# A graph network on one core: norms two octets ahead in the first pass, and 832 packed gathers in the last

## What is computed

```
deg[n]   = number of edges whose source is n
norm[e]  = edge_weight[e] / sqrt(deg[src[e]] * deg[dst[e]])      # first pass, with guards
h[n]     = sum over edges e with dst[e] == n of norm[e] * x[src[e]]   # pass 1
...      # a second pass in source order, a third over q_table, dense layers, a GRU
fwd[n]   = sum over edges of one direction of fwd_table[src]     # pass over fwd_table, 128 wide
bwd[n]   = sum over edges of the other direction of bwd_table    # last pass, 128 wide
out      = layernorm(sums, residual)                             # last turns
```

## Time and profile before

| | |
|---|---|
| median of 3 runs | 7041.7 us (7039.99 to 7042.25) |
| the profiled execution's own time | 7030.23 us |
| its span, first to last instruction | 7028.5 us |
| mean granted TensorE clock | 0.753 of full speed |
| first pass, first to last gather | 277.0 to 1456.4 us |
| last pass, first to last gather | 5862.1 to 6964.0 us |

### The profile page before, as it was taken

The page is one execution under the profiler, slowest core; times in us unless marked ns, Lnnn a source line. Parts: engine busy times, 40 slices in busy tenths (PEclk is TensorE's granted clock), DMA queues, the critical chain, the costliest instruction groups (busy, mean ns, idle before and its releaser), DMA issues. The chain is left out here.

```text
span 7028.5 us, 109321 instructions
## 1 busy us (share of the span) xinstructions
PE 4886.3 (70%) x21773; PEld 3443.5 (49%) x21774; DVE 4004.0 (57%) x9278; ACT 2212.8 (31%) x4093; POOL 4281.9 (61%) x4466
## 2 busy tenths in 40 slices
PE   5455555679999998998888887994555554555553
PEld 3333333447777775676555555553333333333332
DVE  7766666647777775986777775662332222332224
ACT  3333333438888882014333333540000000000000
POOL 1376666727777774004777775006777777777774
PEclk8577667889999998669999999995555555555555
DMA  3133333334333331333333335112221113221222
GB/s 98 44 100 98 97 97 97 105 99 121 104 103 103 104 103 30 99 126 121 105 105 105 105 105 127 34 31 65 65 64 53 53 53 51 52 52 53 52 53 70
DMA packets 292434, 579.79 MB, mean 82 GB/s; under 512 B 86843, under 2 KB 160903, under 8 KB 292169
## 3 DMA queue, kind: packets, MB, share of 16 engines
q0 software_dynamic: 184128, 466.71, 24.9%
q1 hardware_dynamic: 108168, 111.80, 5.2%
HBM read 534.69 MB, written 49.91 MB: 83 GB/s over the span
## 5 line engine op out<-in xcount | busy, mean ns | idle before, releaser
L887 PE MATMUL bank<-ring,oh 128*128 128x128 f32 x3520 | 910.6, 440 | 1094.5 <-DMA ring<-fwd_table,stage_i 558.2
L887 PEld LDWEIGHTS bank<-ring,oh 128*128 128x128 f32 x3520 | 783.5, 328 | 1355.8 <-issue 1355.8
L613 POOL DMA_INDIRECT ring<-h_table,stage_i x880 | 852.4, 969 | 376.9 <-issue 190.4
L631 POOL DMA_INDIRECT ring<-fwd_table,stage_i x880 | 830.6, 944 | 327.0 <-issue 264.8
L631 POOL DMA_INDIRECT ring<-bwd_table,stage_i x880 | 831.8, 945 | 274.3 <-issue 203.6
L1304 ACT ACTIVATE ring<-big 128x889 f16<-128x889 f16 x840 | 873.9, 1041 | 197.8 <-PE bank L965 161.6
L1876 DVE TENSOR_TENSOR acc<-bank,acc 128x1024 f32 x220 | 269.6, 1225 | 987.1 <-PE bank L887 987.1
L965 PE MATMUL bank<-ring,big 128*128 128x445 f16 (+1 forms) x3360 | 773.8, 352 | 0.0
L915 PE MATMUL bank<-big,oh 128*128 128x257 f32 x1072 | 421.9, 559 | 355.5 <-ACT big L1255 219.1
L661 POOL DMA_INDIRECT big<-x_and_degree,stage_i x536 | 507.9, 948 | 187.7 <-issue 118.1
L954 PE MATMUL bank<-ring,oh 128*128 128x256 f32 x1760 | 563.3, 403 | 55.4 <-DVE oh L1845 51.9
(11 more groups left out here) (452 smaller groups left out, 8379.9 us busy)
## 6 DMA issues: line engine op xcount, KB each, us to landing
acc<-places_in_block SPq DMA_DIRECT2D x74, 384.0 KB, 3.5
ring<-h_table,stage_i POOLq DMA_INDIRECT x880, 2.7
ring<-fwd_table,stage_i POOLq DMA_INDIRECT x880
ring<-bwd_table,stage_i POOLq DMA_INDIRECT x880
big<-x_and_degree,stage_i POOLq DMA_INDIRECT x536, 2.8
h_table<-hq SPq DMA_DIRECT2D x50, 128.0 KB, 1.7
x_table<-ring SPq DMA_DIRECT2D x25, 256.0 KB, 2.1
x_turned<-turned SPq DMA_DIRECT2D x25, 256.0 KB, 2.0
```

The costliest lines, as they stand in the source:

```text
L613: pool.indirect_dma_start(out=gbuf[:, u % RING, 0:width], out_offset=None, in_=table, in_offset=bass.IndirectOffsetOnAxis(ap=stage_i[:, v, ...
L631: pool.indirect_dma_start(out=last_rows[:, u, :], out_offset=None, in_=table, in_offset=bass.IndirectOffsetOnAxis(ap=stage_i[:, v, u % RIN ...
L887: mm = pe.matmul(sums[:, ds(b, 1), :].rearrange("p b f -> p (b f)"), oh[:, place, :], last_rows[:, v * RING + u, :], start=False, stop=Tru ...
```

## The change

Four things are altered.

1. **First pass.** `turn` does products and norms for octet k+2 instead of k+1 during octet k. Two octets are prepared before the first turn, and the last full turn is taken out of the loop, because there the last octet has none behind it. ACT no longer waits, ahead of the pass, for POOL to stage five octets.
2. **Prologue.** Twelve of the out-degree batches are put among the 36 weight transposes on PE, one ahead of every three.
3. **Last pass.** Unpadded rows are gathered, 832 instead of 880, into 64 places (`packed`) which take the spare part of `big` and the first columns of `ring`, now one tensor. Tile t uses row t minus its block number. POOL works out that place for each tile (`place_of_tile`) and how many rows must have landed for each group of four (`rows_needed`) during the GRU stage, with ten operations. PE loads eight more registers for each octet, and reads one number for each group and waits for so many rows. SP relays: for each four gathers it waits for their semaphore and adds four to `rows_landed`, then waits for matmuls and frees the next places (`rows_free`). ACT stages four octets ahead.
4. **Indices of the unpadded order.** SP reads them back with two DMAs, PE turns them in seven transposes and ACT copies them to `d_idx` with two operations, all ahead of the node sums.

```diff
-        ring = sb("ring", [P, 2 * RING * (D + 1)])
+        ring = whole[:, BIG:BIG + 2 * RING * (D + 1)]
+        PLACES = 64
+        SETS, ROW_TURNS = PLACES // GROUP, -(-J * P // P) // PLACES
+        packed = whole[:, NX:NX + PLACES * P].rearrange("p (r f) -> p r f", f=P)
...
+            sp.dma_start(flat_win[:, 0:full, :], by_row[0:full * P, :].rearrange("(g p) n -> p g n", p=P)).then_inc(S["row_win_in"], 16)
+            sp.dma_start(flat_win[0:J - full * P, full, :], by_row[full * P:J, :]).then_inc(S["row_win_in"], 16)
...
+            with sp.Fori(0, ROW_TURNS) as i:
+                for g in range(SETS):
+                    sp.wait_ge(gd[g % RING], i * (GROUP * 16 * SETS // RING) + packed_before(g % RING) + GROUP * 16 * (g // RING + 1))
+                    sp.sem_inc(S["rows_landed"], GROUP)
+                    sp.wait_ge(S["mm"], i * PLACES + before_pass(3) + 8 + g * GROUP)
+                    sp.sem_inc(S["rows_free"], 1)
...
-            gathers_by_groups(bwd_dram, before_pass(3))
+            with pool.Fori(0, ROW_TURNS) as i:
+                for u in range(PLACES):
+                    if u % RING == 0:
+                        pool.wait_ge(S["staged"], i * (PLACES // RING) + STAGED[4] + u // RING + 1)
+                    if u % GROUP == 0:
+                        pool.wait_ge(S["rows_free"], i * SETS + u // GROUP + 1)
+                        apart(pool, S["pool_waited"])
+                    pool.indirect_dma_start(out=packed[:, u, :], out_offset=None, in_=bwd_dram,
+                                            in_offset=bass.IndirectOffsetOnAxis(ap=stage_i[:, u // RING % 4, u % RING:u % RING + 1], axis=0)).then_inc(gd[u // GROUP % RING], 16)
...
             for m, (a, _, _) in enumerate(TURN):
+                if m % 3 == 0:
+                    out_degree_batch(CHUNKS[0] + m // 6, m // 3 % 2)
...
+            def packed_pass(slots, shift):
+                def octet(o, v):
+                    pe.load(regs, slots[0:1, ds(o * RING, RING)])
+                    pe.load(row_regs, place_of_tile[0:1, ds(o * RING, RING)])
...
+                        if u % GROUP == 0:
+                            pe.wait_ge(S["one_hot"], n + GROUP)
+                            needed = pe.value_load(rows_needed[0:1, ds(o * 2 + u // GROUP, 1)], min_val=1, max_val=ROW_TURNS * PLACES)
+                            pe.wait_ge(S["rows_landed"], needed)
+                        b = pe.snap(regs[u], min_val=0, max_val=RING - 1)
+                        row = pe.snap(row_regs[u], min_val=0, max_val=PLACES - 1)
...
-            act.wait_ge(S["first_staged"], WIDE)
...
+            with act.Fori(0, ROW_TURNS * PLACES // (4 * RING) - 1) as i:
+                for v in range(4):
+                    act.wait_ge(S["rows_landed"], i * (4 * RING) + (v + 1) * RING)
+                    stage(d_idx, i * (4 * RING) + (v + 4) * RING, v)
...
-                def turn(i, groups, last, places):
+                def turn(i, groups, last, places, ahead):
                     for h in range(groups):
-                        v, at = (h // 2 + 1) % WIDE, i + (h // 2 + 1) // WIDE
-                        if not last:
+                        v, at = (h // 2 + 2) % WIDE, i + (h // 2 + 2) // WIDE
+                        if h // 2 + 2 < ahead:
                             (edge_norms if h % 2 else degree_products)(at, v)
```

More of the change, by code:

```diff
@@ L161, in build @@
         NX = NBE * D
[L162 removed]
+        BIG = 3 * NBE * D // 2
+        whole = sb("big", [P, BIG + 2 * RING * (D + 1)])
+        big = whole[:, 0:BIG]
         x_sb = big[:, 0:NX].rearrange("p (b f) -> p b f", f=D)
@@ L310, in build @@
         zeros = gate_bc
+        rows_needed = gate_rows[0:1, 0, 0:TILES // GROUP].bitcast(I32)
+        row_scratch = [ring[0:1, TC * k:TC * k + TILES] for k in range(2)]
+        assert E <= ROW_TURNS * PLACES * P <= J * P and PLACES - 4 * GROUP >= NB - 1
         pairs_in = lambda a: a.rearrange("p (k n) -> p k n", n=2 * D)
@@ L740, in _ @@
             regs = [pe.alloc_register(f"pe_blk{j}") for j in range(8)]
+            row_regs = [pe.alloc_register(f"pe_row{j}") for j in range(8)]
             slot_regs = regs + [pe.alloc_register(f"pe_blk{j}") for j in range(8, BATCH)]
             pe.sem_inc(S["mm"], 8)
+            pe.sem_inc(S["rows_free"], 3)
             pe.sem_inc(S["sort_mm"], 3)
@@ L783, in turn_windows, with out_degree_batch @@
                         fills += 1
+            def out_degree_batch(i, k):
+                pe.wait_ge(S["dego_oh"], i * 2 + k + 1)
+                for u in range(BATCH):
+                    mm = pe.matmul(bank[7][:, 0:3 * NP], oh_k[k][:, u, :], prod_k[k][:, u, :], start=False, stop=False, skip_group_check=True)
+                mm.then_inc(S["dego_mm"], 1)
             def out_degrees(first, last):
@@ L788, in out_degrees @@
                     for k in range(2):
[L789 to L792, removed]
+                        out_degree_batch(i, k)
             def join_runs():
@@ L896, in scatter_pass @@
                     octet(FULL_TURNS, v)
+            def packed_pass(slots, shift):
+                def octet(o, v):
+                    sums = octet_sums[(v + shift) % 3]
+                    pe.load(regs, slots[0:1, ds(o * RING, RING)])
+                    pe.load(row_regs, place_of_tile[0:1, ds(o * RING, RING)])
+                    pe.wait_ge(S["accd"], o * RING + before_pass(3) + 4 - 2 * RING)
+                    for h in range(2):
+                        pe.matmul(bank[(v + shift) % 3 * 2 + h][:, :].rearrange("p (b f) -> p b f", f=P), zero_row,
+                                  zero_row.unsqueeze(1).to_broadcast([1, 512 // P, P]), start=True, stop=False, skip_group_check=True)
+                    for u in range(RING):
+                        n = o * RING + before_pass(3) + u
+                        place = (2 * (v + shift) + u // GROUP) % 3 * GROUP + u % GROUP
+                        if u % GROUP == 0:
[4 more added lines that the diff above has]
+                        row = pe.snap(row_regs[u], min_val=0, max_val=PLACES - 1)
+                        mm = pe.matmul(sums[:, ds(b, 1), :].rearrange("p b f -> p (b f)"), oh[:, place, :],
+                                       packed[:, ds(row, 1), :].rearrange("p r f -> p (r f)"), start=False, stop=True, skip_group_check=True)
+                        if u % GROUP == GROUP - 1:
+                            mm.then_inc(S["mm"], GROUP)
+                with pe.Fori(0, FULL_TURNS) as i:
+                    for v in range(3):
+                        octet(i * 3 + v, v)
+                for v in range(REST // RING):
+                    octet(FULL_TURNS * 3 + v, v)
             def turn(n, q, src, b):
@@ L1038, in _ @@
             pe.matmul(bank[4][:, 0:D], ones[0:1, :], staged_x[0:1, 1, :], start=True, stop=True).then_inc(S["pe_chain"], 1)
+            pe.wait_ge(S["row_win_in"], 32)
+            for g in range(TG):
+                n = min(P, J - g * P)
+                mm = pe.transpose(bank[6 if g < 4 else 0][:, g % 4 * P:g % 4 * P + n], row_win[0:n, g, :, 0], ident[0:n, 0:n])
+            mm.then_inc(S["pe_chain"], 1)
             node_sums()
@@ L1944, in first_pass @@
                 edge_norms(0, 0)
+                degree_products(0, 1)
+                edge_norms(0, 1)
                 with dve.Fori(0, EXTRA) as i:
                     chain.enter(i, 19)
-                    turn(i, LONG // GROUP, False, True)
+                    turn(i, LONG // GROUP, False, True, WIDE + 2)
                 chain.leave(EXTRA)
-                with dve.Fori(EXTRA, LONG_TURNS) as i:
+                with dve.Fori(EXTRA, LONG_TURNS - 1) as i:
                     chain.enter(i - EXTRA, 10)
-                    turn(i, LONG // GROUP, False, False)
-                chain.leave(LONG_TURNS - EXTRA)
-                turn(LONG_TURNS, RING // GROUP, True, False)
+                    turn(i, LONG // GROUP, False, False, WIDE + 2)
+                chain.leave(LONG_TURNS - 1 - EXTRA)
+                turn(LONG_TURNS - 1, LONG // GROUP, False, False, WIDE + 1)
+                turn(LONG_TURNS, RING // GROUP, True, False, 0)
                 dve.wait_ge(S["accd"], T + 4)
```

32 lines of the change are left out of this document (27 added, 5 removed).

## The result

The changed kernel takes 6926.25 us (median of 3, 6920.03 to 6926.57) against 7041.7; the ratio is 0.9834 with a 95% interval of 0.9811 to 0.9856. The forecast was 6917 with a range of 6895 to 6945. The profiled execution took 6926.25 us with a span of 6924.5, and there the forecast for an execution like the profiled one was 6905, so 21 us are to be explained; 13.8 of them lie between two profiles of this same kernel and are no part of the change.

The account below looks back on a forecast made before the run. No engine always busy: DVE's late norms stalled POOL in the first pass; POOL's gather count set the last. 7030.2 - 68 + 5.5 - 3.8 + 1.0 - 60.0 + 0.3 = 6905.2; median 6917 us, range 6895 to 6945.

Parts of the forecast that it names:

- prologue, first gather: Prologue: out-degree batches among the transposes cut DVE's 10.80 us stall to about 7, -3.8 us (bounds 0 to -10.8).
- stalls of the first pass: First pass: preparing norms two octets ahead removes all of POOL's real stalls, -68 us.
- tail of the first pass: End of first pass: DVE has three octets instead of two behind the last landing, +5.5 us (+4 to +8).
- ahead of the node sums and in them: Before the node sums: reading back unpadded indices by DMAs, transposes and copies, +1.0 us (0 to +2).
- GRU operations: GRU stage: POOL's ten new operations, 10 to 17 us, are covered by other waits; cost 0, up to +3.
- 48 gathers less: Last pass: 48 fewer gathers at 1.25 us each, -60.0 us, with PE staying hidden.
- relay and end: End of last pass: the final matmul waits through SP, +0.3 us for a handover in each direction.
- DVE's turn: First pass, turns with places: 54.7 us falls to DVE's own 50.4, against POOL's 50.0.
- the first rival: First pass: DVE's turn stays the bound, 8 to 25 of the 68 us stay, 6925 to 6942; chance 0.14.
- the prediction's three signs of being wrong: First-pass turns with places over 51 us, POOL waiting for `rows_free`, or PE's last-pass octet over 9.45 us.
- The rule weighed against the change: First pass: two-port DVE operations lock out GpSimd's descriptor writing, so longer gathers would give back part of the look-ahead's gain.
- the 11.5 us added for the median: Whole kernel: the profiled execution lay 11.5 us below the runs' median, so 6905.2 became 6916.7.

Follow-up runs that it names:

- the changed kernel once more: The changed kernel run again with no edit, beside other runs: 6911.27 us, ratio 0.9829 to the kernel before.
- the run with two turns in an iteration: Changed kernel with two turns with places in one iteration of DVE's loop, halving the jumps back: 6911.45 us, ratio 0.9829.
- the late last octet: Changed kernel with the very last octet's products and norms made one octet ahead instead of two: 6905.66 us, ratio 0.9823.

## Why the prediction was right

Against the profile with gathers of the same length as before (the changed kernel once more, span 6910.7), the difference is 117.8 us where 125.0 was forecast. Taken out one at a time, the three parts are worth 57, 56 and 3 us, together 116 of the 119 between the medians. Point by point:

| step | forecast | measured |
|---|---|---|
| prologue, first gather | -3.8 | -4.1 (277.0 to 272.9) |
| stalls of the first pass | -68 | -62.0 (1179.4 to 1117.4) |
| tail of the first pass | +5.5 | +5.3 (110.0 to 115.3) |
| ahead of the node sums and in them | +1.0 | -0.7 |
| GRU operations | 0 | +1.4 in the third pass and the GRU stage, where two profiles of the kernel before differ by 2.9 |
| 48 gathers less | -60.0 | -59.5 (1101.8 to 1042.3) |
| relay and end | +0.3 | +0.5 |

The second and the fourth pass added 1.2 and 0.2, which is scatter.

The mechanism was right, and the term that was mis-sized is DVE's turn. It was taken as 54.7 less the waits for PE above 0.21 us, 50.4. Those waits did go, but idle time at four other places of the turn grew by 0.9 us in all, and the turn is 51.3. With POOL at 50.06 DVE loses 1.2 us in each turn, uses up its slack of two octets by the twelfth, and POOL stalls for 4 to 7 us. The prediction's own sum gives about 5 for such a turn (17 x 1.3 less the slack of 17). So 62 us were gained and not 68: the first rival in a small form, short of the 8 to 25 us that it named, and one of the prediction's three signs of being wrong came up, turns with places that still take over 51 us. The other two did not: POOL never waits for `rows_free`, and PE's octet has 3.7 us to spare. Two slips in the working change nothing: 887 x 1.25 is 1108.8 and not 1111, which belongs to a step of 1.253 (the pass without stalls, in the run with two turns in an iteration, took 1110.5), and turns of 51.5 to 52 would lose 26 to 34 us in 17 turns, not 24 to 32.

The packed pass is bound by POOL's count alone, PE's loads are 0.592 and twice 0.305, inside the bounds, and the relay costs 0.4 us once.

The rule weighed against the change (the Trainium skill, "SBUF — State Buffer", section "SBUF: two separate sides") is about operations that take both of DVE's ports; the prediction carried it over to a denser DVE of any kind, and gathers would then grow. They did not: they have a mean of 947 ns in the first pass both with the look-ahead (the changed kernel once more) and without it. Which of DVE's operations here take both ports no run shows, so the rule itself is neither borne out nor refuted in this direction. In the other direction, DVE operations beside GpSimd's, the trace agrees with a coupling (1.75 us for the cast), and it cost nothing here because DVE had a DMA to wait for.

That the median of 6926.25 lay only 9 above the forecast is in part luck. The sum took off 7 us too much (6905.2 against 6912.4 for the execution with short gathers), the first profiled execution was 13.9 slower than that one, with longer gathers and other scatter, and the 11.5 us added for the median, which came out as about 0 both times that the changed kernel ran, happened to cover most of this. Whether the other executions with times of 6920 us had the longer gathers too, and whether the 11.5 us of before are such executions, is not shown: they have no profile. As a ratio the forecast was 0.9823, inside the measured interval.

## What to carry to other kernels

A wait that is taken away is not all gain: here 4.2 us of waits went in each turn and 0.9 us of idle time grew at other places, so leave a margin where the sum puts two engines within 1% of each other, above all with a loop's jump back, where the engine's own gap repeats in each iteration. Where one engine's step is constant to a few nanoseconds, the number of its instructions times the step is a forecast good to 1%. A small gain from rearranged loops should be looked for over the whole span, since it can be lost in a stage that was not touched.

## What the runs showed of the hardware

- Indirect gathers of one form took a median of 944 ns in some executions and 947 in others of the same code, in all passes alike. Two profiles of one kernel, 944 and 947, differ by 9.1 us in their five gather passes and by 13.8 in their spans of about 6911 and 6925, as much as a small change to such a kernel.
- A jump back in DVE's long loop (five octets of work) stood beside 3.0 to 3.1 us of idle time and, after two instructions, about 1.6 us more. Turns without it took 46.7 us, where the turn with it took 51.3.
- At the end of the GRU stage of the first changed profile two groups of the same eight matmuls took 3.78 us, at a granted clock of 0.50 (1.2 GHz), and the third 1.99 at 1.00 (2.4 GHz). TensorE had been busy for 1.6 of the 6 us before 4690. The kernel before has one slow group there (3.45 us, granted clock 0.57) and then 1.99, and so has the changed kernel once more (3.37); the late last octet has two again. From the first of the three groups to the start of the last are 11.0 us with two slow ones and 8.8 with one.

```profile
4690.69 3.78 PE L1260 MATMUL bank<-wbuf,turned 128*128 128x256 f32 x8 [0.74 <-ACT turned L1540]
...
4696.19 3.78 PE L1260 MATMUL bank<-wbuf,turned 128*128 128x256 f32 x8 [0.87 <-ACT turned L1540]
...
4701.69 1.99 PE L1260 MATMUL bank<-wbuf,turned 128*128 128x256 f32 x8 [1.08 <-ACT turned L1540]
```
